# Cross attention with a router and experts on one core: the last pair of batches in another order on all five engines

## Chip, core and metric

The kernel runs on one core of one Trainium2 chip. The core has a matmul engine (PE, with its weight loads PEld), a vector engine (DVE), an activation engine (ACT), a general engine (POOL, GpSimd) and a queue that starts DMAs (SP). Each engine works through its own list in order, and waits on semaphores for the others. The metric is the time of one execution in microseconds of device time, as the median of several runs. Less is better.

## The reference, cut to what matters

```python
x = x + xattn(layernorm(x), ctx)     # x (32, 112, 256), ctx (32, 375, 192), 8 heads of 64
x = x + ffn(layernorm(x))            # router, top 2 of 8 experts, and one shared expert
# xattn, per batch: q = x Wq, k = ctx Wk, v = ctx Wv, softmax(q k^T / 8) v, then Wout and bout
# shared expert: hs = (x Ws1) * silu(x Ws3);  out = out + hs Ws2
# ffn of the routed experts has the same form, with W1, W3, W2 of the chosen ones
```

## The kernel before

All matrices are split into a high and a low part (names with _hi and _lo), and a product is the sum of high by high, high by low and low by high. ACT makes the high part from the PSUM bank, DVE subtracts it from the bank for the low part.

The function `attention` takes the batches in 16 pairs. A pair has 8 steps s = 0 to 7, each for two heads: steps 0 to 3 are those of its first batch, 4 to 7 those of its second. One step is a chain over four engines:

- `scores(p, s)` on PE (L1377), `maximum` on DVE (L991), two calls of `exponential` on ACT (L732), `reciprocal` on DVE (L1004), `normalise` on POOL (L555);
- `turn_probs` on PE (six transposes, L1403), `high_of_probs` on ACT (L723), `low_of_probs` on DVE (L997);
- `sums` on PE (L1391), `copy_cross` on ACT (L677), `add_cross` and `add_most` on DVE (L1009, L1015), `high_of_sums` on ACT (L682), `low_of_sums` on DVE (L1022).

`scores(s)` waits until both exponentials of step s-1 are done, since they read the same two banks. `sums(s)` waits for `low_of_sums(s-1)` for the same reason. `turn_probs(s)` waits for `low_of_probs(s-1)`.

Beside the steps stand units, which share three PSUM banks in turn: `q1`, `k01` and so on (queries, and keys of a pair of heads of one batch), `v20` and so on (values, whose parts POOL makes in 2.3 us), `w0`, `w1`, `z1` (the output product with Wout; `w1` is that of the batch before, `w0` and `z1` those of the pair). A unit can only be opened when the engine that reads the last unit of the same bank is through. `close` ends two keys or values together. SP stores the results x1, and stages the experts' weights in 16 halves: `load_half`, then `hi_of_piece` on ACT and `split_piece` on POOL three times, then `store_half`.

In the last pair there is no next pair to prepare. There the kernel already computes the shared expert for the first two tiles of 128 rows: `first_statistics`, `first_rstd_of` and `first_normalised` (four DVE operations, L1029), `t0` and `t1` (transposes), `g0` and `g1` (product with Ws3, then Silu on ACT, L705), `u0` and `u1` (product with Ws1, times the Silu, on DVE), `h0` and `h1` (transposes), `y0` and `y1` (product with Ws2), and `r` (the router's product). `second_statistics` and `second_rstd_of` serve rows 512 to 1023. ACT holds one table of functions: Exp and Silu are not in the same one, a plain copy is in both, and between an Exp and a Silu stands an ACT_TABLE_LOAD.

The order of the last pair is written out by hand, once for each engine, behind `rounds(...)`. `LAST_UNITS` must agree with the order in which units are finished, since the semaphores count units, and `LAST_BANK` gives each its bank. Behind it all engines meet at the end of the block (line L239), and `experts` begins with the shared expert of the other tiles (L2150 to L2152).

## Time and profile before

| what | value |
|---|---|
| time, median of 3 runs | 1119.18 us (1118.29 to 1122.79) |
| the profiled execution's own time | 1117.4 us |
| its span, first to last instruction | 1115.7 us |
| PE busy over the span | 1058.5 us, 95% |
| DVE, ACT, POOL busy | 782.6, 685.4, 697.3 us |
| mean granted clock of TensorE | 0.991 of full speed |
| the last pair on PE | 603.4 to 660.6 us |

Times of a row are microseconds from the span's start. A row of a timeline gives start, length, engine, line, operation, what it writes and reads, and in brackets how long the engine was idle just before and what ended that. Instructions of one engine overlap a little, so lengths can add to more than the time between starts.

### The profile page before, as it was taken

What the parts mean: (1) busy time and instruction counts of PE and PEld (TensorE: products, weight loads), DVE (VectorE), ACT (ScalarE), POOL (GpSimd) and SP (SyncE); (2) the same over time, 40 slices, a digit from 0 to 9 for tenths busy, and PEclk for the clock granted to TensorE, in tenths of its full rate; (3) what the DMA queues carried; (4) which work ended last, traced back from release to release, by engine and by line L of the source; (5) the groups of instructions that cost most, each with busy time, mean ns of one, the idle gap of its engine ahead of it and who ended that gap; (6) DMA issues with size and microseconds to landing.
All of it is one profiled execution on the core that took longest, in us unless ns stands there. A gap on an engine that the chain in (4) does not pass through costs nothing. (4 is left out here: it accounts for less than half of the span.)

```text
span 1115.7 us, 25449 instructions
## 1 busy us (share of the span) xinstructions
PE 1058.5 (95%) x7342; PEld 921.0 (83%) x7342; DVE 782.6 (70%) x1969; ACT 685.4 (61%) x1621; POOL 697.3 (62%) x628
## 2 busy tenths in 40 slices
PE   6899999999999999999999789999999999999996
PEld 4788878877888888788778679999988888888885
DVE  4788998899889889988988767776633333333332
ACT  5778777877777777778877764452244434434442
POOL 3888787887878778878878746767033333323233
PEclk9999999999999999999999899999999999999999
DMA  7113133224313321431341359232483345333861
GB/s 216 52 34 102 59 133 107 79 89 137 103 52 119 111 99 64 137 107 48 119 153 65 104 168 334 90 109 97 130 262 63 59 97 124 57 60 55 269 173 14
DMA packets 83985, 124.06 MB, mean 111 GB/s; under 512 B 7904, under 2 KB 48080, under 8 KB 83920
## 3 DMA queue, kind: packets, MB, share of 16 engines
q1 hardware_dynamic: 63664, 99.86, 27.0%
q0 software_dynamic: 11760, 15.15, 7.6%
q10 hardware_dynamic: 8496, 8.22, 2.5%
q8 instruction: 37, 0.61, 0.2%
q14 instruction: 28, 0.23, 0.1%
HBM read 74.44 MB, written 49.68 MB: 111 GB/s over the span
## 5 line engine op out<-in xcount | busy, mean ns | idle before, releaser
L555 POOL TENSOR_TENSOR probs<-probs,first_rows 112x750 f32<-112x750 f32 x128 | 184.0, 1437 | 97.5 <-DVE first_rows L1004 97.3
L1789 POOL DMA_INDIRECT out<-stage,to_row x48 | 74.8, 1559 | 175.8 <-ACT stage L1841 124.8
L2069 DVE TENSOR_TENSOR hT_lo<-banks,hT_hi 128x512 fp32r<-128x512 f32 x63 | 43.5, 691 | 184.3 <-ACT hT_hi L1833 184.3
L732 ACT ACTIVATE probs<-banks,first_rows 112x375 f32<-112x375 f32 x256 | 145.7, 572 | 41.1 <-DVE first_rows L991 25.7
L1391 PE MATMUL banks<-pT,v_both 125*128 125x224 f32 x768 | 117.8, 289 | 21.1 <-DVE oT_lo L1022 19.0
L1391 PEld LDWEIGHTS banks<-pT,v_both 125*128 125x128 f32 x768 | 96.2, 192 | 44.8 <-issue 40.9
L512 POOL TENSOR_TENSOR v_both<-v_raw,v_both 125x512 fp32r<-125x512 f32 x96 | 123.7, 1289 | 7.5
L991 DVE TENSOR_REDUCE first_rows<-banks 112x2 f32<-112x750 f32 x128 | 118.4, 925 | 10.5 <-PE banks L1377 8.8
L508 POOL TENSOR_TENSOR v_both<-v_raw,one 125x512 fp32r<-125x512 f32 x96 | 100.6, 1048 | 21.1 <-ACT v_raw L656 21.1
L1403 PE MATMUL banks<-ident,probs 112*125 112x112 f32 x768 | 108.5, 278 | 2.7 <-POOL probs L555 1.5
L1403 PEld LDWEIGHTS banks<-ident,probs 112*125 112x125 f32 x768 | 96.1, 190 | 16.2 <-issue 11.1
L997 DVE TENSOR_TENSOR pT<-banks,pT 125x672 fp32r<-125x672 f32 x128 | 108.0, 844 | 1.8 <-ACT pT L723 1.6
L723 ACT ACTIVATE pT<-banks 125x672 fp32r<-125x672 f32 x128 | 93.6, 731 | 20.7 <-PE banks L1403 15.9
L2137 PE MATMUL banks<-ring,xr_hi 128*128 x252 | 105.2, 417 | 0.0
L1821 ACT ACTIVATE stage<-banks 128x512 f32<-128x512 f32 x89 | 53.1, 597 | 76.8 <-PE banks L2139 59.9
L2139 PE MATMUL banks<-ring,xr_lo 128*128 x252 | 99.3, 394 | 0.0
L2138 PE MATMUL banks<-ring,xr_hi 128*128 x252 | 99.1, 393 | 0.0
L2059 DVE TENSOR_TENSOR hid<-banks,stage 128x512 f32<-128x512 f32 x89 | 61.5, 691 | 24.3 <-PE banks L2152 11.2
L2226 PE MATMUL banks<-ring,hT_hi 128*128 x504 | 75.4, 292 | 0.8 <-ACT hT_hi L1833 0.8
L1015 DVE TENSOR_TENSOR banks<-banks,o_most 64x112 f32<-64x112 f32 x256 | 71.3, 278 | 6.0
L677 ACT ACTIVATE o_cross<-banks 64x224 f32<-64x224 f32 x128 | 45.3, 354 | 46.4 <-PE banks L1391 43.9
L923 DVE TENSOR_TENSOR k_lo<-banks,k_hi 128x376 fp32r<-128x376 f32 x128 | 67.0, 534 | 5.1 <-ACT k_hi L653 5.0
(284 smaller groups left out, 3078.3 us busy)
## 6 DMA issues: line engine op xcount, KB each, us to landing
w_split_scratch<-stage SPq DMA_DIRECT2D x16, 1536.0 KB, 5.9
ring<-w_split_scratch SPq DMA_DIRECT2D x16, 1536.0 KB, 11.8
stage<-in_L_ffn_W SPq DMA_DIRECT2D x48, 256.0 KB, 2.9
ctx_in<-in_ctx SPq DMA_DIRECT2D x32, 376.0 KB, 3.4
xg<-x_sorted_scratch ACTq DMA_DIRECT2D x59, 136.0 KB, 2.1
x_in<-in_x SPq DMA_DIRECT2D x16, 224.0 KB, 2.9
x_res<-in_x SPq DMA_DIRECT2D x32, 112.0 KB, 4.5
x_scratch<-x SPq DMA_DIRECT2D x32, 112.0 KB, 1.9
```

Source lines behind the costliest of these rows:

```text
L508: pool.tensor_tensor(v_both[b][:, t, :, 0, :], raw, one[0:KR, :].rearrange("p (o q) -> p o q", o=1).to_broadcast([KR, HEADS, DH]), ALU.mul ...
L512: pool.tensor_tensor(v_both[b][:, t, :, 1, :], raw, v_both[b][:, t, :, 0, :].bitcast(F32), ALU.subtract).then_inc(v_ready, 1)
L555: pool.tensor_tensor(probs[:, two, :], probs[:, two, :], inv_sum[:, 2 * s:2 * s + 2].rearrange("p (e o) -> p e o", o=1).to_broadcast([N, 2 ...
L723: act.activation(pT_hi[:, s % 2, :, :, :], PT_BANKS[0:KR, :, 0:KT * N].rearrange("p e (t n) -> p t e n", t=KT), ACT.Copy).then_inc(pT_hi_r ...
L732: act.activation(probs[:, h % 4, :], S_BANKS[0:N, e, 0:M], ACT.Exp, bias=neg_max[:, h:h + 1], accum_out=row_sum[:, h:h + 1]).then_inc(exp_ ...
L991: dve.tensor_reduce(neg_max[:, 2 * s:2 * s + 2], S_BANKS[0:N, :, 0:M], AX.X, ALU.max, negate=True).then_inc(max_ready, 1)
L997: dve.tensor_tensor(pT_lo[:, s % 2, :, :, :], PT_BANKS[0:KR, :, 0:KT * N].rearrange("p e (t n) -> p t e n", t=KT), pT_hi[:, s % 2, :, :, : ...
L1391: mm = pe.matmul(O_BANK[:, e * N2:(e + 1) * N2], v_both[i][:, kt, 2 * m + e, :, :].rearrange("p l d -> p (l d)"), pT[:, s % 2, kt, e, :, : ...
L1403: mm = pe.transpose(PT_BANKS[0:KR, e, kt * N:(kt + 1) * N], probs[:, 2 * (s % 2) + e, kt * KR:(kt + 1) * KR], ident[0:N, 0:N])
L2137: pe.matmul(o, hi, whi, start=(k == 0), stop=False)
L2138: pe.matmul(o, hi, wlo, start=False, stop=False)
L2139: mm = pe.matmul(o, lo, whi, start=False, stop=(k == 1))
```

## The change

The edit touches nothing but the order of the last pair and what follows from it. Each engine's list stands in another order; the units get other banks, and a new list `LAST_OPENED` gives the order in which units are opened where that differs from the order in which they are finished (`t1` is now finished ahead of `v21` and `v11`, though opened behind them). No instruction of PE, DVE, POOL or SP is added or taken away. SP stores the two finished tiles last, behind the last x1.

```diff
-LAST_UNITS = ["q1", "v20", "k31", "k01", "k11", "v21", "v11", "v01", "k21", "t0", "t1", "w1", "g0", "g1", "u1",
-              "u0", "h1", "h0", "r", "y0", "y1", "w0", "z1"]
+LAST_UNITS = ["q1", "k01", "k21", "v20", "k11", "v01", "k31", "t0", "t1", "v21", "v11", "w1", "g0", "g1", "u0",
+              "u1", "h0", "h1", "w0", "y0", "z1", "y1", "r"]
...
@@ the engines' lists: SP
-            sp.wait_ge(unit_done, done_count(p, True, "y1"))
-            sp.dma_start(out_tiles[:, 0:DONE_TILES, :], x1_first[:, 0:DONE_TILES, :]).then_inc(z_first, 16)
             store(2 * p, 0, done_count(p, True, "w0"))
...
+            sp.wait_ge(unit_done, max(done_count(p, True, "y0"), done_count(p, True, "y1")))
+            sp.dma_start(out_tiles[:, 0:DONE_TILES, :], x1_first[:, 0:DONE_TILES, :]).then_inc(z_first, 16)
@@ POOL, the middle
-            run(p, True, "v21")
-            run(p, True, "v11")
+            run(p, True, "v01")
             normalise(p, 3)
             split_piece(p - 1, 0)
-            normalise(p, 4)
-            run(p, True, "v01")
             split_piece(p - 1, 1)
             split_piece(p - 1, 2)
+            normalise(p, 4)
+            run(p, True, "v21")
             normalise(p, 5)
+            run(p, True, "v11")
+            second_rstd_of()
             normalise(p, 6)
@@ ACT, around the Silus
             high_of_sums(p, 2)
+            exponential(p, 6, 0)
+            exponential(p, 6, 1)
             run(p, True, "g0")
             copy_cross(p, 3)
-            exponential(p, 6, 0)
-            exponential(p, 6, 1)
+            run(p, True, "g1")
+            high_of_probs(p, 5)
             high_of_sums(p, 3)
-            high_of_probs(p, 5)
-            run(p, True, "g1")
+            exponential(p, 7, 0)
             copy_cross(p, 4)
-            exponential(p, 7, 0)
@@ PE, the beginning (new order whole)
+            run(p, True, "q1")
+            scores(p, True, 0)
+            run(p, True, "k01")
+            run(p, True, "k21")
+            close(p, True, "k01", "k21")
+            turn_probs(p - 1, 7)
+            sums(p - 1, 6)
+            scores(p, True, 1)
+            run(p, True, "v20")
+            run(p, True, "k11")
+            scores(p, True, 2)
+            close(p, True, "v20", "k11")
+            turn_probs(p, 0)
+            sums(p - 1, 7)
+            turn_probs(p, 1)
+            scores(p, True, 3)
@@ PE, the end (new order whole)
+            turn_probs(p, 6)
+            sums(p, 5)
+            turn_probs(p, 7)
+            run(p, True, "h0")
+            run(p, True, "h1")
+            sums(p, 6)
+            run(p, True, "w0")
+            sums(p, 7)
+            run(p, True, "y0")
+            run(p, True, "z1")
+            run(p, True, "y1")
+            run(p, True, "r")
```

Three places show the move. The first is ACT in the last third of the pair, before. `stage<-banks` is a Silu, `probs,first_rows<-banks,first_rows` one exponential of steps 6 and 7, `o_cross` and `oT_hi` belong to sums, `pT` to the turned probabilities.

```order
L705 ACT_TABLE_LOAD
L705 ACTIVATE stage<-banks 128x512 [waits unit_made]
L677 ACTIVATE o_cross<-banks 64x224 [waits o_made]
L732 ACT_TABLE_LOAD [waits pT_made]
L732 ACTIVATE probs,first_rows<-banks,first_rows 112x375 [waits max_ready]
L732 ACTIVATE probs,first_rows<-banks,first_rows 112x375 [waits pT_made,max_ready]
L682 ACTIVATE oT_hi<-banks 128x112 [waits sum_ready]
L723 ACTIVATE pT<-banks 125x6x112 [waits o_made,pT_made]
L705 ACT_TABLE_LOAD
L705 ACTIVATE stage<-banks 128x512 [waits unit_made]
L677 ACTIVATE o_cross<-banks 64x224 [waits o_made]
L732 ACT_TABLE_LOAD [waits pT_made]
```

The same place of ACT in the changed kernel, whose line numbers are two higher:

```order
L734 ACTIVATE probs,first_rows<-banks,first_rows 112x375 [waits pT_made,max_ready] x2
L707 ACT_TABLE_LOAD
L707 ACTIVATE stage<-banks 128x512 [waits unit_made]
L679 ACTIVATE o_cross<-banks 64x224 [waits o_made]
L707 ACTIVATE stage<-banks 128x512 [waits unit_made]
L725 ACTIVATE pT<-banks 125x6x112 [waits o_made,pT_made]
L684 ACTIVATE oT_hi<-banks 128x112 [waits sum_ready]
L734 ACT_TABLE_LOAD [waits pT_made]
L734 ACTIVATE probs,first_rows<-banks,first_rows 112x375 [waits max_ready]
```

The exponentials of step 6 now stand ahead of both Silus, and only those of step 7 behind them, so two of the four table loads are gone.

The second place is PE around `t0`, before: `ident,first_rows` are the transposes of `t0`, `k_hi,q_hi` to `k_lo,q_hi` the scores of steps 4 (above) and 5 (below).

```order
L1377 MATMUL banks<-k_lo,q_hi 112x376 x2
L1262 MATMUL banks<-ident,first_rows 128x128 [waits unit_hi,first_normed]
L1262 MATMUL banks<-ident,first_rows 128x128 x3
L1377 MATMUL banks<-k_hi,q_hi 112x376 [waits exp_ready,unit_done]
L1377 MATMUL banks<-k_hi,q_hi 112x376
L1377 MATMUL banks<-k_hi,q_lo 112x376 x2
```

And in the changed kernel, from the scores of step 4 to the closing of `v21` and `v11`, behind which the scores of step 5 follow:

```order
L1379 MATMUL banks<-k_lo,q_hi 112x376 x2
L1264 MATMUL banks<-ident,first_rows 128x128 [waits unit_done,first_normed]
L1264 MATMUL banks<-ident,first_rows 128x128 x3
L1237 MATMUL banks<-wv_hi,cT_hi 125x512 [waits unit_hi]
...
L1405 MATMUL banks<-ident,probs 125x112 [waits pT_ready,probs_ready]
...
L1393 MATMUL banks<-pT,v_both 128x224 [waits o_ready,pT_ready]
...
L1237 MATMUL banks<-wv_hi,cT_hi 125x512 [waits unit_done]
...
L1264 MATMUL banks<-ident,first_rows 128x128 [waits unit_done]
...
L1248 MATMUL banks<-wv_hi,cT_lo 125x512 x2
```

Between `t0` and the scores of step 5 stand two value units, the turn of step 2, the sums of step 1 and `t1` now, where before nothing stood.

The third place is the end of DVE's list, before: `first_rows<-first_rows,banks` is `y1`, `x_0` is `w0`, `x_1` is `z1`.

```order
L967 TENSOR_TENSOR first_rows<-first_rows,banks 128x256 [waits unit_made]
L1009 TENSOR_TENSOR o_most<-banks,o_cross 64x224 [waits cross_ready]
L1015 TENSOR_TENSOR banks<-banks,o_most 64x112 [waits most_ready]
L1015 TENSOR_TENSOR banks<-banks,o_most 64x112
L931 TENSOR_TENSOR x_0<-banks,x_res 112x256 [waits x1_stored0,res_biased,unit_made]
L1022 TENSOR_TENSOR oT_lo<-banks,oT_hi 128x112 [waits o_hi_ready]
L931 TENSOR_TENSOR x_1<-banks,x_res 112x256 [waits x1_stored1,res_biased,unit_made]
```

And in the changed kernel, where `first_logits` is `r`:

```order
L1024 TENSOR_TENSOR oT_lo<-banks,oT_hi 128x112 [waits o_hi_ready]
L933 TENSOR_TENSOR x_0<-banks,x_res 112x256 [waits x1_stored0,res_biased,unit_made]
L969 TENSOR_TENSOR first_rows<-first_rows,banks 128x256 [waits unit_made]
L933 TENSOR_TENSOR x_1<-banks,x_res 112x256 [waits x1_stored1,res_biased,unit_made]
L969 TENSOR_TENSOR first_rows<-first_rows,banks 128x256 [waits unit_made]
L984 COPY first_logits<-banks 128x64 [waits unit_made]
```

`y1` and the router's copy now stand behind the last sum of the attention.

## Rows read from the trace of the kernel before

**Rows 1.** Waits of PE, 602 to 662 us: who waited for whom, total, times, longest.

```profile
PE banks L1377 <- ACT probs L732: 4.8, 3, 2.5
PE banks L1391 <- DVE oT_lo L1022: 2.0, 2, 1.5
PE banks L1262 <- DVE first_rows L1029: 1.6, 1, 1.6
PE banks L1282 <- DVE ctx_in L960: 1.3, 1, 1.3
PE banks L2150 <- PEq L239: 1.3, 1, 1.3
PE banks L1208 <- DVE oT_lo L1022: 0.7, 1, 0.7
```

**Rows 2.** Windows: length, busy PE, PEld, DVE, ACT, POOL; granted clock, DMA share, GB/s.

```profile
620.00:625.00 5.00, 1.98 (x16) 1.30 (x14) 4.95 (x10) 2.21 (x5) 3.09 (x3) 0.85 0.01 2
625.00:630.00 5.00, 3.92 (x19) 3.50 (x20) 2.81 (x7) 2.46 (x8) 4.92 (x5) 0.50 0.02 3
645.00:650.00 5.00, 2.35 (x18) 1.86 (x16) 3.95 (x13) 3.93 (x11) 4.22 (x5) 1.00 0.00 0
```

**Rows 3.** Timeline of PE in the last pair: scores 0, scores 5, w1, end of z1.

```profile
603.38 0.42 PE L1377 MATMUL banks<-k_hi,q_hi 64*112 64x376 f32 x2 [1.24 <-ACT probs L732]
...
626.08 0.66 PE L1377 MATMUL banks<-k_hi,q_hi 64*112 64x376 f32 x2 [2.47 <-ACT probs L732]
...
630.49 0.36 PE L1208 MATMUL banks<-wo_hi,oT_hi 128*112 128x256 f32 x1
...
660.31 0.28 PE L1208 MATMUL banks<-wo_lo,oT_hi 128*112 128x256 f32 x1
```

**Rows 4.** Groups of instructions, 602 to 662 us: count, busy us, mean ns, idle before.

```profile
L555 POOL TENSOR_TENSOR probs<-probs,first_rows 112x750 f32<-112x750 f32 x9 | 12.9, 1437 | 10.2 <-DVE first_rows L1004 10.1
L732 ACT ACTIVATE probs<-banks,first_rows 112x375 f32<-112x375 f32 x18 | 10.2, 572 | 3.4 <-DVE first_rows L991 2.3 <-PE banks L1403 1.0
...
L997 DVE TENSOR_TENSOR pT<-banks,pT 125x672 fp32r<-125x672 f32 x10 | 8.5, 849 | 1.7 <-ACT pT L723 1.6
...
L991 DVE TENSOR_REDUCE first_rows<-banks 112x2 f32<-112x750 f32 x8 | 7.5, 932 | 2.0 <-PE banks L1377 1.9
L723 ACT ACTIVATE pT<-banks 125x672 fp32r<-125x672 f32 x10 | 7.3, 734 | 2.8 <-PE banks L1403 2.8
L1015 DVE TENSOR_TENSOR banks<-banks,o_most 64x112 f32<-64x112 f32 x22 | 6.1, 278 | 0.5
...
L1009 DVE TENSOR_TENSOR o_most<-banks,o_cross 64x224 f32<-64x224 f32 x11 | 4.2, 378 | 3.6 <-ACT o_cross L677 3.6
L677 ACT ACTIVATE o_cross<-banks 64x224 f32<-64x224 f32 x11 | 3.9, 354 | 5.7 <-PE banks L1391 5.6
...
L1022 DVE TENSOR_TENSOR oT_lo<-banks,oT_hi 128x112 fp32r<-128x112 f32 x11 | 3.0, 269 | 1.2 <-ACT oT_hi L682 1.1
L682 ACT ACTIVATE oT_hi<-banks 128x112 fp32r<-128x112 f32 x11 | 2.9, 262 | 2.8 <-DVE banks L1015 2.8
```

**Rows 5.** Timeline of ACT around the first Silu.

```profile
634.97 0.26 ACT L682 ACTIVATE oT_hi<-banks 128x112 fp32r<-128x112 f32 x1
635.25 1.28 ACT L705 ACT_TABLE_LOAD   x1
636.54 0.60 ACT L705 ACTIVATE stage<-banks 128x512 f32<-128x512 f32 x1
```

**Rows 6.** Timelines of DVE, POOL and SP: first_normalised, last splits, last sum, last store.

```profile
619.72 3.18 DVE L1029 TENSOR_SCALAR first_rows<-first_rows,mean_var,rstd 128x256 f32<-128x256 f32 x4
...
660.63 0.42 DVE L931 TENSOR_TENSOR x<-banks,x_res 112x256 f32<-112x256 f32 x1 [1.77 <-PE banks L1208]
...
647.32 3.73 POOL L525 TENSOR_TENSOR stage<-stage 128x512 fp32r<-128x512 f32 x3
...
661.08 0.33 SPq L480 DMA_DIRECT2D x_scratch<-x  x1
```

**Rows 7.** DMA issues of the whole span: count, KB each, median us to landing.

```profile
w_split_scratch<-stage SPq DMA_DIRECT2D x16, 1536.0 KB, 5.9
```

More of the change, by code:

```diff
@@ L60, in opened_of @@
 def opened_of(p, last):
-    return LAST_UNITS if last else without_w1(OPENED, p)
+    return LAST_OPENED if last else without_w1(OPENED, p)
 def count_of(p, last, name, kinds):
@@ L627, in _ @@
             split_piece(p, 2)
[L628 removed]
+            add_bout(1, p + 1)
             pool.wait_ge(second_rstd, 1)
@@ L819, in _ @@
             exponential(p, 1, 1)
+            run(p, True, "k21")
             high_of_sums(p - 1, 6)
-            run(p, True, "k01")
+            run(p, True, "v20")
             run(p, True, "k11")
             high_of_probs(p, 0)
+            exponential(p, 2, 0)
             copy_cross(p - 1, 7)
-            exponential(p, 2, 0)
             exponential(p, 2, 1)
             high_of_sums(p - 1, 7)
-            run(p, True, "v21")
-            run(p, True, "v11")
             high_of_probs(p, 1)
@@ L1126, in _ @@
             low_of_probs(p - 1, 6)
+            first_statistics()
             run(p, True, "q1")
-            first_statistics()
+            maximum(p, 1)
             reciprocal(p, 0)
-            maximum(p, 1)
-            run(p, True, "k31")
+            run(p, True, "k01")
             add_cross(p - 1, 6)
+            low_of_probs(p - 1, 7)
+            reciprocal(p, 1)
             add_most(p - 1, 6)
-            low_of_probs(p - 1, 7)
+            run(p, True, "k21")
             low_of_sums(p - 1, 6)
-            reciprocal(p, 1)
             maximum(p, 2)
-            run(p, True, "k01")
-            run(p, True, "k11")
             low_of_probs(p, 0)
@@ L1333, in run @@
                     pe.wait_ge(ctx_lo_ready[0], p + 2)
-                if name == ("k31" if last else "k21"):
+                if name == ("k01" if last else "k21"):
                     pe.wait_ge(ctx_lo_ready[1], p + 1)
```

124 lines of the change are left out of this document (54 added, 70 removed).

## The prediction

> **What bounds the kernel.** Over the whole span PE is busy 95%, so I look only at where PE stands still in the stretch that the edit touches. The waits of PE from 602 to 662 us [rows 1] are the first view. Six kinds stand there. The fifth, 1.3 us, is the meeting at the end of the block. The others add to 4.8 + 2.0 + 1.6 + 1.3 + 0.7 = 10.4 us. The longest, 2.5 us, is scores 5 waiting for the exponentials of step 4; the 1.6 us just ahead of it is `t0` waiting for `first_normalised`.
>
> The windows come second [rows 2]. From 620 to 630 us the granted clock is 0.85 and then 0.50, that is 1.2 GHz of 2.4. PE was busy only 1.98 of 5 us ahead of that. From 645 to 650 us PE is as idle, 2.35 of 5, and the clock stays at 1.00. So idleness of this size may cost the clock, and need not. What the clock cost is read from the timeline [rows 3]: from scores 5 at 626.08 to `w1` at 630.49, 4.4 us for four pieces of work (scores, sums, turn, transposes) that take about 2.5 us elsewhere in the same timeline. With the slow `t0` ahead of it that is 2.0 us lost.
>
> So PE's work in the pair at full clock is 660.6 - 603.4 = 57.2, less the waits behind 603.4 (10.4 - 1.2 = 9.2), less 2.0, which gives 46.0 us. That is what the change keeps. What it can gain at most is 10.4 + 2.0 = 12.4 us, or 1.1% of the time, if PE never waited again. The attention is a chain of steps over four engines, so that can't be reached: the sums of one step can't follow those of the step before in less than `copy_cross` 0.35, `add_cross` 0.38, `add_most` 2 x 0.28, `high_of_sums` 0.26 and `low_of_sums` 0.27 [rows 4], 1.8 us and some 0.4 us of hand-overs.
>
> **The change, part by part.** Nearly everything moves, so the sum is a walk: I took each engine's new list in its order, gave every instruction its mean length [rows 4] and each hand-over 0.05 to 0.15 us as the timelines show it, and noted where PE stands. The start is PE free at 603.38 - 1.24 = 602.1 us [rows 3].
>
> *The beginning.* `q1` now goes ahead of scores 0 and fills the 1.2 us for which PE had waited on the last exponentials. Scores 0 start at 603.4 as before. Then new waits come. On ACT `q1` stands ahead of `high_of_probs` of the pair before, so the turn of its step 7 waits 0.3 us. `v20` and `k11` get the banks of `q1` and `k01`, whose DVE readers now stand behind `first_statistics` and a maximum: 0.2 and 0.7 us. The sums of step 7 wait 0.3 us. The turn of step 1 now stands ahead of scores 3 and needs `low_of_probs` of step 0, which DVE reaches at 614.5 us: 1.4 us, with 0.1 behind it. That is 3.0 us of waits where PE had none, against 1.2 gained. At scores 3 the changed kernel is about 1.1 us behind the old one, counted in work done.
>
> *The middle.* `first_normalised`, 3.18 us on DVE [rows 6], starts about 618.2 us instead of 619.7: `low_of_router` has left the place ahead of it. Scores 4 wait 0.5 us. `t0` still waits 1.6 us, since scores 4 come early too. But the next piece that needs an exponential is now five pieces later [the second place in the order]. The maximum of step 4 stands behind two more unit reads on DVE and ends at 625.0, and exponential 4 ends at 626.6 us, later than before; PE reaches scores 5 only 0.7 us ahead of it. So 2.5 us become 0.7, and at the end of scores 5 (627.4 us) PE has done the sums of step 1 and `t1` in addition: about 1.2 us ahead. No stretch of five microseconds has PE as idle as 620 to 625 was, so I take the clock to stay at 2.4 GHz. That is worth the 1.8 us that fell behind 626.
>
> *The Silus.* Four table loads of 1.28 us become two [rows 5], 2.6 us less on ACT. Scores 7 waited 1.05 us before, since exponential 6 stood behind two loads and a Silu; now step 6 is through first, and scores 7 don't wait. What is late next is step 7: its exponentials stand behind both Silus and the way back, and end at 641.3 us. `copy_cross` of step 4 stands between them, so that `low_of_sums` of step 4 ends at 643.4, and the sums of step 5 wait 1.6 us, as long as the 1.5 us of before. So the loads are worth about 1 us on the path and not 2.6.
>
> The row has the load at 635.25, 0.02 us behind the instruction ahead, and the Silu 0.01 us behind its end [rows 5]. The Trainium skill, page "ScalarE: Activation LUTs", section "What ACT_TABLE_LOAD costs", gives about 1.28 us for the load and about 1.38 us of drain with it, 2.66 us a switch. By that, two switches less would be 5.3 us of ACT, not 2.6. The length of the load agrees with the trace; of the drain it shows nothing, so the sum leaves it out.
>
> *POOL.* `v21` and `v11` (2.3 us each) now stand around `normalise` 5, and `second_rstd_of` ahead of `normalise` 6. In the walk `normalise` 6 ends at 639.1 us, and PE asks for it at 641.2. This is cover of 2.1 us; were it gone, each microsecond beyond it would be PE's.
>
> *The tail.* Scores 6 wait 0.3, sums 4 0.6, sums 5 1.6, `h1` 1.2 (for `u1`, which stands on DVE behind `add_most` 5), sums 7 0.9, and `z1` 0.9 us for the last `low_of_sums`, with `y0` as its only cover. Behind `z1` come `y1` and `r`, which need nothing that is late.
>
> *The end.* Before, the last matmul ended at 660.59 [rows 3], DVE's sum ended at 661.05, SP issued the last store until 661.41 [rows 6], and the experts began 1.3 us after PE's end [rows 1]. Now DVE's last is the router's copy, 0.2 us, and SP's stores are issued ahead of it. I take the 0.5 us from SP's issue to the first matmul as it is: 0.04 + 0.23 + 0.5 = 0.8 instead of 1.3 us, 0.5 us gained. If instead the 0.86 us from DVE's end to the first matmul stay, it is 0.2 us.
>
> *The last half of the weights.* Its splits take 3.73 us [rows 6], its store 5.9 us [rows 7], and the block can't end before it has landed. In the walk the splits start at 643.9 behind `normalise` 7, the store lands about 654 us, and the block ends near 659: hidden, by some 4 us.
>
> **The sum.** PE waits 3.0 + 0.5 + 1.6 + 0.7 + 0.3 + 0.6 + 1.6 + 1.2 + 0.9 + 0.9 = 11.3 us. With the work of 46.0 us that is 602.1 + 46.0 + 11.3 = 659.4 us. In the walk itself PE ended at 657.9, since it counted each piece at its shortest; the 1.5 us between them are what a piece costs more that starts after a wait, and a part of that hides in the next wait. I take the middle, 658.7, which is 1.9 us ahead of 660.6. With 0.5 us at the end the span loses 2.4 us: 1115.7 becomes 1113.3, the profiled execution's own time 1117.4 becomes 1115.0. The median of the runs stands 1.8 us above that one, so I forecast 1119.2 - 2.4 = **1116.8 us**, own range 1115.0 to 1118.5. Behind the meeting all is as before, only earlier.
>
> **The rivals.**
>
> *The clock falls in the middle as before.* The waits of 1.4 and 1.6 us (613 and 620 us) lie apart, but before, 1.6 us and then 2.5 did it. What it cost then, 2.0 us [rows 2, 3], would be lost again: 1118.8. Chance 0.15.
>
> *Slower: the clock falls in the tail too.* From 642 to 654 us the walk has PE waiting 1.6, 1.2, 0.9 and 0.9 us. The tail of before had waits of 1.5, 1.3 and 0.7 at full clock [rows 1, 2], which speaks against it. If it falls for as long as in the middle of before, some 6.6 us, half of these are lost, 3.3 us; with the 2.0 of the middle this gives 1116.8 + 5.3 = 1122.1, slower than before by 3 us. It decides from a total loss of 2.4 us on. Chance 0.07.
>
> *The late waits are shorter.* Sums 5, `h1`, sums 7 and `z1` wait for places in the lists of ACT and DVE, not for the bare chain. If `copy_cross` 4 comes ahead of the first exponential's wait and `u1` ahead of `add_cross` 5, half of these 4.6 us go, and with the lower end of the piece costs, 0.8 us, that is 3.1 us more: 1113.7. Chance 0.17.
>
> *The end of the block waits for POOL and SP.* If `normalise` 7 slips by over 4 us, the store of the last half ends the block, at its start plus 3.7 + 0.4 + 5.9 us. At 2 us over it would eat the gain: 1118.8. Chance 0.03.
>
> **How the numbers follow.** The forecast has the remaining 0.58. The range takes in the first, the third and most of what lies about them: 1113.0 to 1120.3, and leaves out the slower rival and the far end of the third. A measurement of this kernel can tell about 0.5%, 5.6 us, from no change. Faster by more, below 1113.6, needs the third rival at its full size or beyond: 0.11. Slower by more, above 1124.8, needs the clock in both places and something else: 0.05. The rest, 0.84, is within.
>
> **What the changed profile would show.** PE from `q1` at 602 us without a wait ahead; a wait of over 1 us at the turn of step 1; `t0` still waiting 1 to 2 us for `first_normalised`, and scores 5 under 1 us; granted clock 1.00 from 620 to 630 us; two table loads instead of four in the pair, and no wait at scores 7; sums 5 still waiting over 1 us; the experts' first matmul at 659.5 instead of 661.9. The prediction is wrong if the clock falls in this stretch, if turn 6 waits for POOL, or if PE's waits add to under 8 or over 14 us.

## The result and the profile after

| | before | changed |
|---|---|---|
| time, median of 5 runs | 1119.21 us (1118.29 to 1122.79) | 1111.67 us (1109.80 to 1113.51) |
| ratio to before, 95% interval | | 0.9929 (0.9911 to 0.9946) |
| profiled execution, own time and span | 1117.4 and 1115.7 us | 1110.78 and 1109.0 us |
| mean granted clock | 0.991 | 0.992 |

The change took 7.5 us off the median. The forecast was 1116.8 us with a range from 1113.0: the sign was right, the time came out below the range.

The pair starts 1.7 us sooner in the new profile although nothing ahead of it was edited, and the stage of the experts differs by some us from one profile to another (453.8 us in before, 455.4 in the changed kernel, 458.3 in its next run). So I compare one stretch within each profile, called **the stretch** below: from PE's start of the sums of step 5 of the pair before to the experts' first matmul. Before it is 661.91 - 601.23 = 60.68 us [rows 1], with the start from the same timeline; after it is 653.64 - 599.53 = 54.11. That is 6.57 us of the 6.7 by which the spans differ.

The first view is PE's timeline of the changed kernel, and these are all the pieces in it that PE waited for in the pair, as [rows 1] is for before. Columns: start, length, engine, line, operation, what it writes and reads, and in brackets the idle time ahead and what ended it.

```profile
608.19 0.44 PE L1237 MATMUL banks<-cT_hi,wk_hi 128*128 128x376 f32 x1 [0.43 <-DVE k_lo L925]
...
612.74 0.88 PE L1405 MATMUL banks<-ident,probs 112*125 112x112 f32 x6 [1.16 <-DVE pT L999]
...
634.56 0.90 PE L1393 MATMUL banks<-pT,v_both 125*128 125x224 f32 x6 [0.17 <-DVE oT_lo L1024]
...
638.87 0.90 PE L1393 MATMUL banks<-pT,v_both 125*128 125x224 f32 x6 [1.38 <-DVE oT_lo L1024]
...
641.82 0.66 PE L1284 MATMUL banks<-ident,ctx_in 128*128 128x128 f32 x4 [0.87 <-DVE ctx_in L962]
...
645.30 0.90 PE L1393 MATMUL banks<-pT,v_both 125*128 125x224 f32 x6 [0.75 <-DVE oT_lo L1024]
...
648.27 0.38 PE L1210 MATMUL banks<-wo_hi,oT_hi 128*112 128x256 f32 x1 [0.66 <-DVE oT_lo L1024]
...
653.64 0.36 PE L2152 MATMUL banks<-firstT_hi,w_hi 128*128 128x256 f32 x1 [0.58 <-PEq L241]
```

In order they are `k11`, the turn of step 1, sums 4, sums 5, `h1`, sums 7, `z1`, and the meeting at the end of the block. There is a gap of 22 us without a wait between 612 and 634, just where before had 1.64, 2.47 and 0.49 us. The waits add to 6.0 us against 11.7 before (meeting included); the other 0.8 us of the 6.57 is PE's work. That is a difference of two things: the slow clock of before took about 2 us, and PE's pieces in the new order take some 1.2 us more at full clock. The windows with the clock:

```profile
620.00:625.00 5.00, 4.89 (x38) 3.96 (x37) 4.57 (x10) 4.78 (x12) 5.00 (x5) 1.00 0.01 3
625.00:630.00 5.00, 5.00 (x36) 4.26 (x35) 3.93 (x10) 3.57 (x12) 4.92 (x5) 1.00 0.73 271
645.00:650.00 5.00, 4.04 (x32) 3.87 (x33) 3.22 (x10) 0.95 (x3) 0.00 (x0) 1.00 0.69 243
```

These windows of after answer to [rows 2] (PE's busy time is the second number, the granted clock the third from the end). PE is busy 4.89 and 5.00 of 5 us from 620 to 630, where it was 1.98 and 3.92, and the clock stays at 1.00.

Why the middle has no wait is seen on DVE and POOL. First DVE of after, then POOL of after:

```profile
615.98 1.38 DVE L1031 TENSOR_SCALAR first_rows<-first_rows,mean_var,rstd 128x256 f32<-128x256 f32 x4
```

```profile
614.40 1.44 POOL L557 TENSOR_TENSOR probs<-probs,first_rows 112x750 f32<-112x750 f32 x1
617.96 1.04 POOL L510 TENSOR_TENSOR v_both<-v_raw,one 125x512 fp32r<-125x512 f32 x1 [2.12 <-ACT v_raw L658]
```

`first_normalised` takes 1.38 us, and took 3.18 [rows 6]. POOL stood idle from 615.84 to 617.96 while it ran. Before, POOL ran without a gap beside it:

```profile
618.47 1.29 POOL L512 TENSOR_TENSOR v_both<-v_raw,v_both 125x512 fp32r<-125x512 f32 x1
619.72 1.04 POOL L508 TENSOR_TENSOR v_both<-v_raw,one 125x512 fp32r<-125x512 f32 x1
620.84 1.27 POOL L512 TENSOR_TENSOR v_both<-v_raw,v_both 125x512 fp32r<-125x512 f32 x1
```

My walk took the 3.18 us over as they were. That is the first theory: **POOL beside DVE made these four operations long, and the new order takes POOL away from them.** The rivals: it is the place in DVE's list, or the Silus carry the gain.

One part of the middle has no run of its own. No experiment puts the pieces that now stand between `t0` and scores 5 back on PE alone, so what they are worth is not measured.

### The profile page after: what moved, and what is told of

It is laid out like the page before. It is cut to its first block and busy times, and to the rows that moved or that the text cites. A ratio compares the mean times of both kernels' runs of the same rounds, so it can differ in the third digit from the quotient of the medians.

```text
span 1109.0 us, 25447 instructions
## 1 busy us (share of the span) xinstructions
PE 1058.8 (95%) x7342; PEld 921.5 (83%) x7342; DVE 779.6 (70%) x1969; ACT 682.3 (62%) x1619; POOL 697.2 (63%) x628
```

## The experiments

Runs came from several chips. The kernel before took 1119 to 1131 us on them, most of the difference in the experts' stage, so times are compared by their ratio to before on the same chip, and the stretch decides. Expectations that count from scores 0 mean a stretch shorter by 2.15 us in orders of before (58.53 in before itself) and by 2.18 in changed ones (51.93). Those that count from the turn of step 1 start from 40.90 us in the changed kernel. All of them:

| kernel | stretch, us | ratio to before (95%) |
|---|---|---|
| before | 60.68 | 1 |
| changed | 54.11 | 0.9929 (0.9911 to 0.9946) |
| changed, two more runs | 54.11, 54.11 | 0.9924 (0.9898 to 0.9949), 0.9941 (0.9921 to 0.9960) |
| changed, a Silu ahead of exponential 6 | 57.15 | 0.9974 (0.9957 to 0.9991) |
| changed, two sums on POOL beside DVE | 56.91 | 0.9968 (0.9948 to 0.9989) |
| changed, four memsets there | 54.66 | 0.9945 (0.9924 to 0.9966) |
| changed, q1 behind scores 0 | 55.38 | 0.9957 (0.9936 to 0.9977) |
| changed, splits late | 61.18 | 0.9999 (0.9986 to 1.0012) |
| changed, three waits filled | 53.54 | 0.9936 (0.9913 to 0.9959) |
| the same and a new tail | 52.97 | 0.9939 (0.9920 to 0.9959) |
| before, exponential 6 first | 60.95 | 1.0019 (1.0001 to 1.0038) |
| before, exponential 6 and sums 3 first | 60.85 | 0.9989 (0.9972 to 1.0005) |
| before, v21 and v11 late on POOL | 65.97 | 1.0069 (1.0045 to 1.0094) |
| the same and exponential 6 first | 66.40 | 1.0040 (1.0024 to 1.0055) |
| before, v11 late | 63.11 | 1.0004 (0.9983 to 1.0025) |
| before, v11 late and splits early | 60.73 | 0.9972 (0.9955 to 0.9989) |

### The changed kernel again

> The changed kernel once more, as the base for the others of this group. If the gain belongs to the order, the median is 1110 to 1113.5 us; the four operations of first_normalised on DVE take about 1.4 us together as in the first profile (3.18 us before), and the granted clock is 1.00 from 620 to 630 us. If the first profile was a lucky one, first_normalised varies from run to run and lies between 1.4 and 3.2 us here.

> The changed kernel once more, beside the two runs that start from the kernel before. Ratio to before 0.993, from the sums of step 5 of the pair before to the experts 54.1 us, first_normalised 1.38 us. Where POOL, DVE and PE repeat as in the runs so far, all these numbers come within 0.1 us; what differs from chip to chip is the stage of the experts.

Both came out as expected: medians of 1110.94 and 1112.29 us, and `first_normalised` at 4 x 0.41 and 4 x 0.40 us. The stretch is 54.11 us in all three profiles, so a few tenths in it mean something, while the times of one kernel spread over 4 us. That holds for a kernel whose clock stays up; no kernel in which it falls was profiled twice.

### The Silus, alone and taken out

```diff
 the kernel before, ACT
+            exponential(p, 6, 0)
+            exponential(p, 6, 1)
             run(p, True, "g0")
             copy_cross(p, 3)
-            exponential(p, 6, 0)
-            exponential(p, 6, 1)
```

> The kernel before, with one edit on ACT alone: both exponentials of step 6 ahead of g0, so that two of four table loads go. Theory A (the gain came from DVE's first_normalised running at full speed beside an idle POOL, and from the clock that then stayed up; the loads are worth 1 us): 1 us faster than before, near 1118, the wait of 1.05 us at scores 7 gone, the slow clock from 620 to 630 us still there. Rival B (the following Silus are the gain, as the title of the change says): 4 us or more faster, 1115 or below.

```diff
 the changed kernel, ACT
+            run(p, True, "g0")
             exponential(p, 6, 0)
             exponential(p, 6, 1)
-            run(p, True, "g0")
             copy_cross(p, 3)
             run(p, True, "g1")
```

> The changed kernel with one edit on ACT alone: g0 ahead of the exponentials of step 6 again, so four table loads. Theory A: exponential 6 ends 3 to 4 us later than in the changed kernel, scores 7 wait for it some 1 to 2 us, and the time is 1 to 2.5 us above the changed kernel's. Rival B: 4 us or more above it, most of the gain gone.

Alone it gave nothing: the stretch is 0.27 us longer, so neither theory A's 1 us nor rival B's 4 came. Out of the changed kernel it cost 3.04 us of stretch, between theory A's 2.5 and rival B's 4. By the medians on the same chip it is 5.6 us (1116.49 against 1110.94), where rival B asked for 4 or more. So in the changed kernel the Silus' order is worth more than theory A gave it. PE of before with exponential 6 first, then PE of changed with the Silu first:

```profile
640.60 0.90 PE L1391 MATMUL banks<-pT,v_both 125*128 125x224 f32 x6 [2.36 <-DVE oT_lo L1022]
```

```profile
634.90 0.42 PE L1379 MATMUL banks<-k_hi,q_hi 64*112 64x376 f32 x2 [1.44 <-ACT probs L734]
```

```profile
635.00:640.00 5.00, 4.71 (x20) 3.35 (x21) 4.25 (x14) 4.92 (x9) 3.15 (x4) 0.66 0.39 124
```

The last is the window behind that wait. In the first, the wait at scores 7 had gone, and sums 4 waited 2.36 us instead: `copy_cross` 3 stood behind the load and the Silu. In the second, scores 7 wait 1.44 us, and the window behind has the clock at 0.66: 1.55 us of the 3.04 are waits, and 1.49 us are PE's pieces taking longer. The next run takes sums 4 out of the way:

```diff
 the kernel before, ACT, whole order
             exponential(p, 6, 0)
             exponential(p, 6, 1)
             copy_cross(p, 3)
             high_of_sums(p, 3)
             run(p, True, "g0")
             high_of_probs(p, 5)
             run(p, True, "g1")
```

> The kernel before with exponential 6 ahead of the first Silu, as in the second experiment, but copy_cross 3 and high_of_sums 3 ahead of that Silu too. In the second experiment the wait at scores 7 (1.05 us) had gone, and one of 2.36 us stood at sums 4, since copy_cross 3 came behind the table load and the Silu. Theory A (the Silus' order alone gave nothing in before because sums 4 took over the wait): sums 4 waits 0.3 to 0.8 us, the clock stays at 1.00 from 642 to 646, and the stretch from scores 0 to the experts is 56.5 to 57.6 us, against 58.8 in that experiment and 58.5 in before; in time 1 to 2 us under before. Rival B (the pace is set by the bare chain of steps, whichever piece of ACT stands first): the wait goes on to sums 5 or turn 6, and the stretch stays over 58 us.

Rival B held. Sums 4 waited 0.47 us, but the turn of step 6 waited 0.82 and sums 5 1.22, and the stretch was 60.85. ACT's load on the way back to Exp starts at 643.11, against 643.13 in before [rows 5 has the first load there]. ACT of this run, exponential 6 and `high_of_sums` 3:

```profile
636.77 0.58 ACT L732 ACTIVATE probs<-banks,first_rows 112x375 f32<-112x375 f32 x1 [1.72 <-DVE first_rows L991]
639.43 0.26 ACT L682 ACTIVATE oT_hi<-banks 128x112 fp32r<-128x112 f32 x1 [1.05 <-DVE banks L1015]
```

The 2.6 us of two loads came back as 2.8 us in which ACT stood for DVE, 1.72 for the maximum of step 6 and 1.05 for `add_most` 3. So in the order of before the Silus are not worth their loads.

### POOL beside first_normalised

```diff
 the changed kernel, POOL
             first_rstd_of()
             normalise(p, 2)
+            for n in range(2):
+                pool.tensor_tensor(xn[:], x_in[:], x_in[:], ALU.add).then_inc(filler, 1)
+                pool.wait_ge(filler, n + 1)
             run(p, True, "v01")
```

> The changed kernel with two tensor_tensor of 112x512 added on POOL (results not used) behind normalise 2, where POOL stood idle while DVE ran first_normalised. Theory A: the four operations of first_normalised take 2.5 to 3.2 us instead of 1.4, t0 waits 1 to 2 us, and the time is 1 to 3 us above the changed kernel's, more if the clock falls. Rival C (POOL has nothing to do with it; the operations were slow before for another reason, as the DMAs or the place in memory): 1.4 us stays, and the time is within 0.7 us of the changed kernel's, as v01 on POOL is only 0.6 us later.

With four `pool.memset(xn[:], 0.0)` in the place of the two sums:

> The changed kernel with four memsets of a 112x512 tile on POOL beside first_normalised, where the run with two 112x512 sums on POOL had made those four DVE operations 4.59 us long instead of 1.38. A memset writes but reads nothing. Theory A (POOL and DVE share the way to SBUF, whatever POOL does): first_normalised takes over 2.5 us again, t0 waits over 0.8 us for it and the stretch from turn 1 to the experts is 1 us or more longer than the 40.9 us of the changed kernel. Rival B (only POOL's reads, or operations with two inputs, stand in DVE's way): first_normalised stays at 1.4 us, t0 waits 0 to 0.2, and the stretch stays within 0.5 us of 40.9. By both the values of POOL behind the memsets may come later, which could cost up to 1 us at sums 1 in either case; so the length of the four DVE operations decides, not the time.

The view by tile gives the count of the four operations, their shortest, median and longest in ns, and their first and last start. In order: before, after, with the two sums, with the four memsets.

```profile
L1029 DVE TENSOR_SCALAR first_rows<-first_rows,mean_var,rstd x4: 400/795/1423, 619.7 to 622.5; 128x256 f32<-128x256 f32 x4
```

```profile
L1031 DVE TENSOR_SCALAR first_rows<-first_rows,mean_var,rstd x4: 405/409/410, 616.0 to 616.9; 128x256 f32<-128x256 f32 x4
```

```profile
L1035 DVE TENSOR_SCALAR first_rows<-first_rows,mean_var,rstd x4: 1009/1195/1420, 614.9 to 618.1; 128x256 f32<-128x256 f32 x4
```

```profile
L1035 DVE TENSOR_SCALAR first_rows<-first_rows,mean_var,rstd x4: 461/688/691, 617.6 to 619.2; 128x256 f32<-128x256 f32 x4
```

Alone each takes 0.41 us. Beside the sums of 1.08 us and the parts of `v01` (1.04 and 1.26 us) each takes 1.0 to 1.4, beside memsets of 0.59 us most take 0.69 and one 0.46: the length of one is about that of POOL's piece, as if the two engines took turns. The sums made `first_normalised` 4.59 us long, more than the 3.18 of before, `t0` waited 2.53 us, and the stretch grew by 2.80. The parts of `v01` on POOL did not come later (18.49 us behind the start of the stretch, 18.43 in the changed kernel), so the wait comes from DVE. The clock stayed at 1.00. By the medians this run is 4.6 us over the changed kernel, and its profile is that of the fastest of its ten executions (1111.28 us, median 1115.50), so 2.80 may be a mild case. The memsets gave 2.29 us, a wait of 0.23 and 0.55 us of stretch: below what theory A had put down, by size, but a POOL that only writes holds DVE up too, which rules rival B out. The rival "the place in DVE's list" falls as the cause of the length, since DVE's list was that of the changed kernel in both runs.

The Trainium skill, page "SBUF — State Buffer", section "Who interferes with whom", says that the two engines share one pair of ports, that a `tensor_scalar` in a two-port mode needs it, that an operation with two inputs in SBUF collides with a GpSimd instruction that reads SBUF, and that whoever starts first holds the pair for the whole instruction. The lengths above agree with that; which mode the `tensor_scalar` ran in, no run here shows. The prediction did not draw on this page.

### The same from the side of before

```diff
 the kernel before, POOL
-            run(p, True, "v21")
-            run(p, True, "v11")
             normalise(p, 3)
+            run(p, True, "v21")
+            run(p, True, "v11")
```

> The kernel before with one edit on POOL: normalise 3 ahead of the parts of v21 and v11, so that POOL stands idle while first_normalised runs on DVE; the lists of PE, DVE, ACT and SP are those of before. Theory A (in before the four operations of first_normalised and low_of_router were long because POOL ran beside them, and this fed the fall of the clock): first_normalised 1.4 us instead of 3.18, low_of_router 0.15 instead of 0.79, t0 waits 0 to 0.3 instead of 1.64, scores 5 waits 1.3 to 2.2 instead of 2.47, and the stretch from scores 0 to the experts is 2.0 to 4.5 us shorter than the 58.5 of before, 4 if the clock stays at 1.00 from 620 to 630 and 2 if it falls. In time 1.8 to 4 us under before. Rival B (the length belongs to the place in DVE's list or to the values themselves, and the sum of exponential 4 sets the pace in any case): first_normalised over 2.5 us or, if it is short, scores 5 wait longer by as much, and the stretch stays within 0.7 us of 58.5. Rival C (the values of POOL come too late): a new wait on PE at close v21,v11 or at turn 4.

> The kernel before with both edits: normalise 3 ahead of v21 and v11 on POOL, and exponential 6 ahead of the first Silu on ACT. The Silus' order alone had given nothing in before (58.8 against 58.5 us for the stretch), while taking it out of the changed kernel cost 3.0. Theory A (the two help each other, since the first keeps the clock up where the second's gain was lost in a fall of the clock): the stretch is 1 us or more shorter than with POOL's edit alone, the clock is at 1.00 from 620 to 650, scores 7 doesn't wait. Rival B (the Silus' order is worth nothing in the lists of before, whatever the clock does, since sums 5 waits longer by what scores 7 waits less): the stretch is within 0.5 us of that with POOL's edit alone, and sums 5 waits over 2 us.

`first_normalised` came down to 4 x 0.41 us as theory A had it, and the kernel got slower by 0.7%. ACT and then PE of the first of these two:

```profile
624.44 0.60 ACT L656 ACTIVATE v_raw<-banks 125x512 f32<-125x512 f32 x1 [5.02 <-POOL v_both L512]
```

```profile
627.28 0.66 PE L1377 MATMUL banks<-k_hi,q_hi 64*112 64x376 f32 x2 [6.30 <-ACT probs L732]
```

The copy of `v01` needs a buffer `v_raw` that `v21` held until POOL was through, and exponential 4 stood behind that copy. None of my theories had this place; rival C was the nearest. With the Silus' order on top it was the same picture (6.31 us at scores 5, 2.37 at sums 4). The stretch was within 0.5 us of the other's, as rival B had it, but sums 5 waited 0.63 us and not over 2, and by the medians this kernel was 0.3% faster. So this pair of runs told nothing on whether the two help each other. The next run leaves `v21` where it was:

```diff
 the kernel before, POOL
             run(p, True, "v21")
-            run(p, True, "v11")
             normalise(p, 3)
+            run(p, True, "v11")
```

> The kernel before with only the parts of v11 moved behind normalise 3 on POOL; v21 stays where it was. The earlier edit, with both moved, showed first_normalised at 4 x 0.41 us, but ACT's copy of v01 stood 5.0 us for POOL (the buffer v_raw is there twice, and v21 held it), with exponential 4 behind it. Now v21 is through at 619.7 us, when ACT gets to that copy, and POOL is idle from then to about 622. Theory A (the overlap with POOL is what made first_normalised long, and the wait at scores 5 and the fall of the clock hang on it): first_normalised 1.4 us, the maximum of step 4 at about 622.0 instead of 623.8, t0 waits 0 to 0.3, scores 5 waits 1.5 to 2.3, ACT doesn't wait over 0.6 us at the copy, and the stretch from scores 0 to the experts is 1.7 us (clock falls as before) to 4 us (clock stays) shorter than 58.5. Rival B (DVE isn't what sets the middle of before): the stretch stays within 0.7 us of 58.5 though first_normalised is short.

The middle did as theory A had it: `first_normalised` 4 x 0.40 us, no wait at `t0`, 2.38 at scores 5, clock 1.00 to 645. At scores 7 the kernel was 3.6 us ahead of before, counted from scores 0 (33.22 against 36.81 us). Scores 5 still waited as long as in before (2.47), so a short `first_normalised` does not take that wait away; in the changed kernel, where other pieces stand ahead of scores 5, it is gone. Then the run lost all of it and more. PE, ACT and POOL of this run, and the window behind:

```profile
643.70 0.90 PE L1391 MATMUL banks<-pT,v_both 125*128 125x224 f32 x6 [3.73 <-DVE oT_lo L1022]
645.83 1.60 PE L1403 MATMUL banks<-ident,probs 112*125 112x112 f32 x6 [0.80 <-POOL probs L555]
```

```profile
642.46 0.63 ACT L687 ACTIVATE stage<-stage 128x512 fp32r<-128x512 f32 x1 [2.10 <-DMA stage<-in_L_ffn_W]
```

```profile
642.96 1.43 POOL L518 TENSOR_TENSOR x_res<-x_res,bout_sb 112x256 f32<-112x256 f32 x2 [6.49 <-DMA x_res<-in_x]
```

```profile
645.00:650.00 5.00, 4.21 (x21) 4.17 (x20) 4.32 (x15) 2.48 (x5) 4.92 (x6) 0.50 0.01 3
```

ACT stands for the next half of the experts' weights, with `high_of_sums` 4 behind it, and POOL for `x_res`, loaded behind that half, with `normalise` 6 behind it. PE waits 3.73 us for sums 5 and the clock is at 0.50 from 645 to 655. The stretch is longer than before, so neither theory A nor rival B held. SP can load a half only when the last one is split by POOL, stored and out of the buffer.

### The splits and the load behind them

```diff
 the kernel before with v11 late, POOL
             normalise(p, 4)
-            run(p, True, "v01")
             split_piece(p - 1, 1)
             split_piece(p - 1, 2)
+            run(p, True, "v01")
```

> The kernel before with v11 behind normalise 3 on POOL, as in the last experiment, and in addition the splits 1 and 2 of the weights' half ahead of v01. The last experiment was 3.6 us ahead of before at scores 7, and lost it all at sums 5, which waited 3.73 us: ACT stood 2.1 us for the next half of the weights (loaded only when the last one is split, stored and out of the buffer) with high_of_sums 4 behind it, and POOL 6.5 us for x_res, loaded behind the same half. Theory A (this chain of split, store and load is the next bound, and the changed kernel gains because it moves the splits ahead too): the splits end 2.3 us sooner, the load is issued at about 635.2 instead of 637.6 (with scores 0 at 601.7), ACT waits under 0.3 us at hi_of_piece 0, sums 5 waits 1.3 to 2.2 instead of 3.73, turn 6 under 0.3, and the stretch from scores 0 to the experts is 55 to 57.3 us, against 61.0 in the last experiment and 58.5 in before. In time 1.5 to 3.5 us under before. Rival B (something else holds sums 5): the wait stays over 3 us and the stretch over 60.

ACT had no wait for the half, the turn of step 6 none, and sums 5 waited 1.51 us, all as theory A had it. The stretch, 58.59 us from scores 0, was not the 55 to 57.3 expected: the clock fell at scores 5, with the same wait (2.37 us) and the same lists up to there as in the run before, where it had stayed (that run was on another chip). It fell again behind 645 us (0.89, then 0.77). The windows from 620 to 625 of that run and of this one:

```profile
620.00:625.00 5.00, 2.62 (x23) 2.18 (x22) 4.05 (x10) 3.58 (x11) 4.48 (x4) 1.00 0.02 5
```

```profile
620.00:625.00 5.00, 2.94 (x14) 2.52 (x15) 3.17 (x6) 2.68 (x9) 4.92 (x5) 0.66 0.01 3
```

By the median of ten runs this kernel is 0.28% faster than before, 2.5 us in 1130.8 and inside theory A's 1.5 to 3.5, while v11 late alone was level. The profiled execution took 1129.69 us, 1.4 over the median, and its stretch is that of before. Then the same step taken back in the changed kernel:

```diff
 the changed kernel, POOL
-            split_piece(p - 1, 1)
-            split_piece(p - 1, 2)
             normalise(p, 4)
             run(p, True, "v21")
             normalise(p, 5)
             run(p, True, "v11")
+            split_piece(p - 1, 1)
+            split_piece(p - 1, 2)
```

> The changed kernel with the splits 1 and 2 back behind v11 on POOL, where their end comes at about 633 us instead of 625.5; all else as in the changed kernel, so that normalise 4 and v21 come sooner by 2.5 us. Theory A (the place of the splits, which the prediction had as a move without a price, sets when the next half can be loaded): the half is there at about 643.8, ACT waits about 5 us for it at hi_of_piece 0, copy_cross 5 stands behind it, a wait of 4 to 5.5 us stands at sums 6 or the pieces ahead of it, and the stretch from the sums of step 5 of the pair before to the experts is 57.5 to 60 us instead of 54.1; in time 3.5 to 6 us over the changed kernel, with a fall of the clock near 650. Rival B (the load has enough slack in the changed kernel): no wait over 1.4 us anywhere, and the stretch within 0.7 us of 54.1.

It takes the whole gain: ratio 0.9999, stretch 61.18, with a clock of 0.57 from 650 to 655. SP of the changed kernel (store of a half, then the load of the next), and then SP, ACT and PE of this one:

```profile
625.51 0.40 SPq L423 DMA_DIRECT2D w_split_scratch<-stage  x1
631.39 0.81 SPq L416 DMA_DIRECT2D stage<-in_L_ffn_W  x2
```

```profile
635.77 0.40 SPq L423 DMA_DIRECT2D w_split_scratch<-stage  x1
641.62 0.81 SPq L416 DMA_DIRECT2D stage<-in_L_ffn_W  x2
```

```profile
646.61 1.15 ACT L689 ACTIVATE stage<-stage 128x512 fp32r<-128x512 f32 x2 [6.21 <-DMA stage<-in_L_ffn_W]
```

```profile
649.79 1.12 PE L1284 MATMUL banks<-ident,ctx_in 128*128 128x128 f32 x4 [6.87 <-DVE ctx_in L962]
```

Store and load are 5.9 us apart in both, and the first piece can be read 5.0 us after the load is issued. In the changed kernel that makes 636.4 us, and ACT gets to the piece at 638.30: 1.9 us of slack. In before it is 638.73 + 5.0 = 643.7 for a piece read at 645.54, 1.8 us of slack. So an order that is over 1.8 us faster ahead of this point gains nothing more unless the splits move too. The wait is theory A's, but larger than it had it (ACT 6.2 us instead of 5, PE 6.87 and not 4 to 5.5, the stretch 7.1 us longer and not 3.4 to 5.9). PE's wait stood at `h1`, the piece ahead of sums 6.

### q1 ahead of scores 0

```diff
 the changed kernel, PE (and on ACT behind high_of_probs(p - 1, 6))
-            run(p, True, "q1")
             scores(p, True, 0)
+            run(p, True, "q1")
```

> The changed kernel with q1 behind scores 0 again on PE, and on ACT behind high_of_probs of step 6 of the pair before. The prediction gave q1 ahead of scores 0 a price of 1.2 us: it fills the time for which PE waits on the last exponentials. Theory A (it is worth that where it stands): PE again waits about 1.2 us ahead of scores 0, and from the last piece ahead of scores 0 to the experts' first matmul the stretch is 1.0 to 1.5 us longer than in the changed kernel; scores 0 itself starts at the same place, so from scores 0 on the stretch is longer by the 1 us of q1's work. Rival B (the 1.2 us only come back as shorter waits behind): the turn of step 1, which waited 1.16 us for DVE, waits under 0.3 us and the experts begin within 0.4 us of the changed kernel. In time that is +1.2 against 0, under the spread of the runs, so the stretch in the profile decides. The granted clock stays at 1.00 to 654 us by both.

The stretch is 1.27 us longer, and every wait behind is the one of the changed kernel (0.43, 1.16, 1.38, 0.86 and so on). The price of 1.2 us stands, theory A.

Taken out of the changed kernel one at a time, the Silus' order, the idle POOL, the splits and `q1` cost 3.0, 2.8, 7.1 and 1.3 us. That is 14.2 us, more than the 6.57 gained, so none of these figures is that part's share of the gain.

### The waits that are left

```diff
 PE:
+            run(p, True, "v01")
             turn_probs(p, 1)
             scores(p, True, 3)
-            run(p, True, "v01")
 ACT:
+            high_of_sums(p, 4)
             high_of_probs(p, 6)
-            high_of_sums(p, 4)
 DVE:
+            run(p, True, "u1")
             add_cross(p, 5)
             add_most(p, 5)
-            run(p, True, "u1")
```

> The changed kernel with three of its left waits filled: v01 ahead of the turn of step 1 on PE (it waited 1.16 us for low_of_probs), high_of_sums 4 ahead of high_of_probs 6 on ACT (sums 5 waited 1.38), and u1 ahead of add_cross 5 on DVE (h1 waited 0.87). Theory A (these waits stand for places in the lists, and not for the bare chain): turn 1 waits under 0.3 us, sums 5 under 0.9, h1 under 0.2, and from scores 0 to the experts the stretch falls from 51.9 us to 49.5 to 50.5. Rival B (the chain of steps sets the pace): the waits move on to sums 6, sums 7 and z1, and the stretch stays within 0.7 us of 51.9. In time 1109.5 against 1111.5, if the clock does as in the changed kernel.

On top of that, PE ends with `sums 6, w0, y0, sums 7, y1, z1, r`, and DVE reads them in that order, with `h0` read ahead of `low_of_probs` 7:

> The kernel with the three waits filled and, in addition, its tail in another order: w0 and y0 ahead of sums 7, then y1 and only then z1 and r, with the readers on DVE in the same order. Theory A (the last waits, 0.75 us at sums 7 and 0.66 at z1, stand only for want of work ahead of them): both fall under 0.2 us, and the stretch from scores 0 to the experts is 0.6 to 1.2 us shorter than without the new tail, 3 us shorter than in the changed kernel. Rival B (with PE through sooner, the end of the block waits for the store of the last half of the weights, or for DVE's last readers): PE's waits fall, but the meeting at the end of the block grows from 0.58 us to over 1.2, and nothing is gained. 1108.8 us by A, 1109.8 or more by B.

Rival B held in the first: the turn of step 1 waited 0.23 us, sums 5 0.70, `h1` not at all, as planned, but scores 3, sums 6 and two more took 0.71, 0.80, 0.20 and 0.18, and the stretch gained 0.57 us. The new tail gained 0.57 again: sums 7 no longer waited, `z1` waited 1.09 us for DVE's reading of `w0`, and the meeting stayed at 0.59. So neither theory held there in full: the gain is just under theory A's 0.6, and both edits together gained 1.1 us and not 3. Both are 0.6% faster than before, and by their intervals can't be told from the changed kernel. What is left looks like the chain of the steps for the most part; these two runs don't prove it.

## Why the prediction was wrong

**What bounds it, and the direction.** Right. The most to be gained was put at 12.4 us; 6.57 came.

**The beginning.** Waits of 3.0 us were forecast, 1.59 came: `k11` 0.43 for 0.7, the turn of step 1 1.16 for 1.4, and the small ones at the turn of step 7, `v20` and sums 7 not at all. `q1`'s 1.2 us was right. The text has the kernel 1.1 us behind at scores 3; 3.0 of waits less 1.2 gained would be 1.8, and it gives no working for the difference.

**The middle: the step that failed.** "`first_normalised`, 3.18 us on DVE [rows 6], starts about 618.2 us": the length was carried over from a place where POOL worked beside it to one where POOL is idle. It took 1.38 us. From it hung `t0` 1.6, and behind that scores 5 0.7 and scores 6 0.3, 2.6 us in all, and none of them came. (Scores 4's 0.5 us, which didn't come either, needs the maximum of step 3, and that stands ahead of `first_normalised` on DVE: a smaller miss of its own.) `first_normalised` also started 0.5 us sooner than in the walk. With that start and 3.18 us, `t0` would still have waited about 1.1 us, an estimate from 615.98 + 3.18 and PE's being free at 618.03. The run with the sums on POOL shows the step at work: 4.59 us, and 2.53 at `t0`. The maximum of step 4 ended 2.1 us sooner than in the walk, after the shift of 1.7 us is taken out. The trace of before held the hint: of the four equal operations in these 3.18 us the shortest took 0.40 and the longest 1.42.

**The clock.** Right that it stays at 1.00 from 620 to 630. My reason, no five microseconds as idle as those of before, was right here. But the two runs with v11 late show that the same wait may or may not bring it down. A wait of 2.53 us left it at 1.00 in the run with the sums on POOL, and one of 1.44 brought it down in the run with a Silu first. So the runs don't say what chance the rival deserved. One reading was off: the `t0` called slow takes 0.66 us in before and 0.66 at full clock in the changed kernel, so nearly all of the 2.0 us lost lies behind 626.

**The Silus.** Four loads became two, scores 7 don't wait and sums 5 still wait 1.38 us (1.6 forecast). The value, about 1 us, was not what either order showed: nothing in that of before, 3.0 in the changed one, of which half is slower work at the fallen clock.

**POOL.** `normalise` 6 had ended at 635.66, and the turn of step 6, at 636.68, didn't wait: a cover of 1.0 us instead of 2.1. What I left without a price is the move of the splits. I costed the last half's store, 5.9 us, as hidden, and it was. That the load of this half hangs on the splits ahead stood nowhere in the working, and moving them back costs 7.1 us. The walk came out without that wait only because the edit had moved them; that was luck.

**The tail.** 0.6 + 1.6 + 1.2 + 0.9 + 0.9 = 5.2 us forecast, 0.17 + 1.38 + 0.87 + 0.75 + 0.66 = 3.83 measured. Each place was right, and each was put too high.

**The end.** 1.32 became 0.58: 0.74 gained, 0.5 forecast.

**The sum.** Waits of 5.4 us instead of 11.3 make 5.9 us less: 1.4 in the beginning, 3.1 in the middle and 1.4 in the tail. By the prediction's own sign, waits under 8 us, it was wrong, and its sign of `t0` waiting 1 to 2 us failed too. Work, from PE free to its last matmul, was 47.2 us, not the 45.3 that the middle of my two figures stands for: 1.9 us more. Even the 46.0 of full-clock work was 1.2 too low, and this hid part of the miss. Together 4.0 us, and PE's end was 3.9 us sooner than forecast, at the same start. With the 0.24 at the end the stretch is 4.2 us shorter than forecast; the medians are 5.1 us under it. The third rival, shorter late waits, went the right way but blamed the tail, which held 1.4 of it.

## What to carry to other kernels

Before the lengths of one order are carried to another, ask for each DVE operation with a wide spread what POOL did beside it in the trace, and what it will do beside it now; the shortest of equal operations was here the length alone. A wait removed brings forward everything behind it, so look up the next thing with a time of its own, here a load that can only start when another engine has freed its buffer, and count its slack: it caps the gain. One part of such a change, tried alone, may give nothing or a loss (the Silus nothing, POOL's order between nothing and 0.7% slower) and still be needed in the whole.

## What the runs showed of the hardware

A DVE `TENSOR_SCALAR` of 128x256 takes 0.40 us alone and mostly 0.7 to 1.4 beside POOL. An operation of 128x16 with two inputs in SBUF, `low_of_router`, took 0.15 to 0.17 us alone and 0.79 beside POOL. DVE and POOL of before with v11 late:

```profile
617.32 0.79 DVE L1048 TENSOR_TENSOR wr_split<-wr,wr_split 128x16 fp32r<-128x16 f32 x1
```

```profile
616.79 1.29 POOL L512 TENSOR_TENSOR v_both<-v_raw,v_both 125x512 fp32r<-125x512 f32 x1
```

It ends at 618.11, 0.03 us behind POOL's operation, as if it had stood until that was through. The same may be at work in the loop, where line L893 of before, an equal `TENSOR_SCALAR` of 112x256, has a mean of 1168 ns over 32 operations; that wasn't tried.

The clock fell in one run and stayed in another at the same wait (2.37 and 2.38 us), with equal lists ahead. Elsewhere it stayed at a wait of 2.53 us and fell behind one of 1.44. What decides between them stays open.
